# A decoder layer on one core: attention rounds rebuilt on head-centred values, with the decays computed a round earlier

## The reference

```
x1 = norm(x + out_proj(norm(scan(x))))        # selective scan, 16 states a channel
x2 = norm(x1 + attention(x1, ctx))            # 4 heads of 32, causal within a sequence of 64
out = norm(x2 + experts(x2))                  # 8 experts, the best 2 of them per token
```

```
log_D = cs[s] - cs[t] + ig[t]   (t <= s, else -inf),   D = exp(log_D - rowmax)
C     = (q @ k.T / sqrt(32)) * D
h     = (C / max(|sum_t C|, exp(-rowmax))) @ v
h     = (h - mean(h)) * rsqrt(var(h) + 1e-5) * outnorm
```

## Time and profile before

| | us |
|---|---|
| median of 3 runs | 712.76 |
| the three runs | 712.76, 706.27, 712.81 |
| the profiled execution | 705.29 |
| its span | 703.7 |
| PE, DVE, ACT, POOL busy | 539.9, 436.6, 319.9, 359.9 |
| mean granted TensorE clock | 0.869 |

### The profile page before, as it was taken

How to read it: one execution, slowest core, us unless ns; L and a number is a source line. 1 busy time by engine, 2 the same in 40 slices (tenths; PEclk the granted TensorE clock), 3 DMA queues, 4 the chain that set the end, 5 groups by cost and what they waited for, 6 DMA issues and landing times.

```text
span 703.7 us, 10811 instructions
## 1 busy us (share of the span) xinstructions
PE 539.9 (77%) x3387; PEld 381.7 (54%) x3387; DVE 436.6 (62%) x912; ACT 319.9 (45%) x700; POOL 359.9 (51%) x293
## 2 busy tenths in 40 slices
PE   3689999899889797686463879797876689899800
PEld 0234435445344456575353768676665568899800
DVE  1599999999999861676748366656451612212155
ACT  2475575866757444122133345454532423333327
POOL 1497978988779651215516163535352533322341
PEclk9999999999999996555565799998998989999955
DMA  4324435355354513733441735461615247789594
GB/s 148 150 99 148 176 122 189 123 170 177 116 190 146 183 50 67 133 67 62 88 113 36 184 133 157 140 234 37 220 52 187 80 151 244 244 276 287 199 240 122
DMA packets 83320, 104.52 MB, mean 149 GB/s; under 512 B 40784, under 2 KB 64592, under 8 KB 83136
## 3 DMA queue, kind: packets, MB, share of 16 engines
q1 hardware_dynamic: 74576, 90.99, 42.4%
q0 software_dynamic: 4320, 8.92, 3.7%
q10 hardware_dynamic: 4368, 3.93, 2.0%
HBM read 91.48 MB, written 12.34 MB: 148 GB/s over the span
## 4 chain that ended last, share of the span: by engine, by line
issue 27%; PE 20%; DVE 16%; POOL 13%; DMA 10%; SPq 3%; ACT 2%; another core or an unknown queue 1%; ACTq 0%; POOLq 0%; DVEq 0%
POOL hc L634 7%; PE pB L1054 6%; DVE h L1489 6%; DMA wslot<-in_expert_w 5%; PE pq L1067 4%; PE py L809 3%; DVE u L1480 3%; POOL y_dram L737 2%; POOL xg_dram L728 2%; ACT x_all L1439 1%; PE pC L988 1%; DMA y_dram<-dx,xin 1%; POOL dx L621 1%; DMA x_all<-y_dram 1%; PE pq L862 1%
## 5 line engine op out<-in xcount | busy, mean ns | idle before, releaser
L634 POOL TENSOR_TENSOR hc<-h,Crep 128x1024 f32<-128x1024 f32 x64 | 149.5, 2355 | 20.8 <-DVE h L1489 19.8
L737 POOL DMA_INDIRECT y_dram<-dx,xin x71 | 68.7, 968 | 153.4 <-ACT dx L1361 144.3
L1054 PE MATMUL pB<-Crep,wslot 128*128 128x256 f32 (+1 forms) x556 | 118.2, 358 | 21.9 <-DMA wslot<-in_expert_w 10.5
L809 PE MATMUL py<-hc,ident 128*128 128x512 f32 x256 | 121.1, 600 | 6.2 <-POOL hc L634 6.2
L1054 PEld LDWEIGHTS pB<-Crep,wslot 128*128 128x128 f32 x556 | 90.6, 204 | 38.6 <-DMA wslot<-in_expert_w 13.1
L1480 DVE TENSOR_TENSOR u<-dx,pC 128x1024 f32<-128x1024 f32 x64 | 77.1, 1205 | 11.7 <-PE pC L798 11.6
L1784 DVE TENSOR_TENSOR Crep<-u,pB 128x512 f32<-128x512 f32 x35 | 24.1, 687 | 85.3 <-PE pB L1054 48.0
L809 PEld LDWEIGHTS py<-hc,ident 128*128 128x128 f32 x256 | 47.3, 191 | 52.4 <-issue 38.8
L1489 DVE TENSOR_TENSOR_SCAN h<-pB,u 128x1024 f32<-128x1024 f32 x32 | 73.1, 2284 | 0.8 <-ACT pB L1187 0.6
L1489 DVE TENSOR_TENSOR_SCAN h<-pa,u 128x1024 f32<-128x1024 f32 x32 | 73.1, 2283 | 0.0
L1784 DVE TENSOR_TENSOR u<-u,pB 128x512 f32<-128x512 f32 x36 | 24.8, 688 | 77.8 <-PE pB L1054 47.1
(11 more groups left out here) (224 smaller groups left out, 950.8 us busy)
## 6 DMA issues: line engine op xcount, KB each, us to landing
wslot<-in_expert_w SPq DMA_DIRECT2D x46, 768.0 KB
Crep<-c_dram SPq DMA_DIRECT2D x64, 512.0 KB, 3.7
h<-m_dram SPq DMA_DIRECT2D x16, 256.0 KB
xin<-xg_dram SPq DMA_DIRECT2D x25, 130.0 KB
cT_st<-in_ctx_T SPq DMA_DIRECT2D x8, 256.0 KB, 4.0
dx<-in_ctx_T SPq DMA_DIRECT2D x8, 256.0 KB, 4.9
delta<-in_ctx_tok SPq DMA_DIRECT2D x32, 64.0 KB
hc<-y_dram SPq DMA_DIRECT2D x8, 256.0 KB, 8.4
```

The lines of the kernel that those rows point to most:

```text
L634: nc.gpsimd.tensor_tensor(hc[:, K % 4], h[:, K % 3], Crep[:, K % 4].rearrange("p a t -> p (a t)"), ALU.mult).then_inc(hc_done, 1)
L737: nc.gpsimd.indirect_dma_start(out=y2_dram, out_offset=bass.IndirectOffsetOnAxis(ap=xin[:, i % NX, a, D:D + 1].bitcast(i32), axis=0), in_= ...
L809: last = nc.tensor.matmul(py[:], ident[:], hc[:, K % 4, i * CH:(i + 1) * CH], start=False, stop=(K % STEPS == STEPS - 1 and i == 1))
L1054: last = nc.tensor.matmul(bank[:, o * a * P:(o + 1) * a * P], wslot[:, i % NW, stage * F + f * P:stage * F + (f + 1) * P], xgT[i % 2][:, 0 ...
```

## The change

- **Centred values.** The mean of a head is taken out of the values before they are weighted. PE multiplies ctx by a constant centring matrix (`hcenter`, `head_values`), ACT copies the result into `V1` (`copy_values`). The direct loads of the values (`load_v`, four DMAs a chunk) are gone. Since the weighted values are centred already, `normalize` needs no mean: it multiplies by `outnorm` straight from PSUM, ACT squares from PSUM (`square_heads`), and the two row factors are put together in small operations.
- **x2 on ACT.** The last step of `normalize` (four 128x128 operations on DVE, L1645) becomes one small DVE operation (`nma`) and four activations on ACT (`normal_x2`).
- **Decays one round ahead.** `weight_decay(c + 2)` stands at the end of round c on ACT, after `z2_scale` and `normal_x2`. Before, `weight_decay(c + 1)` stood in its first half. For chunks 0 to 4 the gate is added inside the exponential, as a bias: 16 activations of 64 columns in place of one of 1024 and of the DVE addition. For chunks 5 to 7 DVE still adds.
- **First chunk in the last scan chunk.** Chunk 0's buffers move into the expert weights' space (`flatw`). Its ctx and maxima are loaded during the last scan chunk, its mask is made by POOL between the last two `weigh_state`, and its scores and weighted values stand earlier on PE.
- **Weights at the front.** `weights` stands directly behind the first parts of `normalize` on DVE, and the scores and weighted values come sooner on PE. Logits and ranks move from a bank of `pC` into `pa`, and no longer wait for `normalize` to have read `pC`.

```diff
+            def load_m(c):
+                sp.wait_ge(m_stored, 16 * (1 if c < GATED[0][1] else 2))
+                if c == 1:
+                    sp.wait_ge(hc_done, STEPS * NCH)
+                elif c:
+                    sp.wait_ge(causal_done, c)
...
+                    if c + 1 == NCH and k == 1:
+                        load_heads(0)
+                    if c + 1 == NCH and k == 6:
+                        store_m(0)
+                    if c + 1 == NCH and k == 7:
+                        load_m(0)
...
             for c in range(NCH):
                 for k in range(STEPS):
                     weigh_state(STEPS * c + k)
+                    if c + 1 == NCH and k == 6:
+                        start_mask(0)
...
+            def head_values(c):
+                pe.wait_ge(heads_loaded, 16 * (c + 1))
...
+                for b in range(TB):
+                    last = nc.tensor.matmul(pC[:, 0, b * P:(b + 1) * P], cTc[late(c)][:, b * P:(b + 1) * P], hcenter[:],
+                                            start=True, stop=True)
...
             def turn_x2(c):
                 pe.wait_ge(x2_done, c + 1)
                 if c:
-                    pe.wait_ge(x2T_copied, c)
+                    pe.wait_ge(ranks_read, c)
...
             def logits(c):
...
-                pe.wait_ge(hv_done, min(c + 2, NCH))
...
             def weight_decay(c):
-                act.wait_ge(log_decay_done, c + 1)
-                if c:
+                act.wait_ge(causal_done, c + 1)
+                act.wait_ge(g_made, 1 if c < GATED[0][1] else 2)
...
-                nc.scalar.activation(Dm, lmask, ACT.Exp).then_inc(D_done, 1)
+                if c >= ADDED:
+                    act.wait_ge(gates_added, c - ADDED + 1)
+                    nc.scalar.activation(Dm[1], lmask[1], ACT.Exp).then_inc(D_done, 1)
+                    return
+                for m in range(TB * H):
+                    last = nc.scalar.activation(Dm[late(c)][:, m * S:(m + 1) * S], lmask[late(c)][:, m * S:(m + 1) * S], ACT.Exp,
+                                                bias=g_sb[:, c * TB * H + m:c * TB * H + m + 1])
...
+            def normal_x2(c):
+                act.wait_ge(x2_shift_done, c + 1)
+                act.wait_ge(z2_rstd_done, c + 1)
+                for b in range(TB):
+                    last = nc.scalar.activation(x2_rows(c)[:, b], z2[:, b], ACT.Identity, scale=rstd[:, b:b + 1],
+                                                bias=nma[:, b:b + 1])
...
                 if mid:
                     z2_scale(c)
+                    normal_x2(c)
+                if c + 2 < NCH:
+                    weight_decay(c + 2)
                 expert_units(second[2:])
...
-                mid(0)
+                mid(0, 1, 2)
                 if front:
-                    add_gates(c + 1)
-                mid(1, 2, 3, 4)
+                    weights(c + 1, 0)
+                rt(0)
+                mid(3, 4)
                 expert_units(first[0:1])
-                mid(5, 6)
+                mid(5, 6, 7)
...
-                mid(8)
+                mid(8, 9)
                 rt(7)
-                if front:
-                    weights(c + 1, 1)
+                mid(10)
+                if ADDED <= c + 2 < NCH:
+                    add_gates(c + 2)
                 expert_units(second[0:1])
                 rt(8)
-                mid(9)
+                mid(11)
                 rt(9)
-                mid(10)
+                mid(12)
                 expert_units(second[1:2])
```

More of the change, by code:

```diff
@@ L1643, in normalize @@
                     dve.wait_ge(z2_rstd_done, c + 1)
-                    for b in range(TB):
-                        last = nc.vector.tensor_scalar(x2_rows(c)[:, b], z2[:, b], mv[:, b, 0:1], rstd[:, b:b + 1],
-                                                       ALU.subtract, ALU.mult)
-                    last.then_inc(x2_done, 1)
+                    nc.vector.scalar_tensor_tensor(nma[:], mv[:, :, 0], -1.0, rstd[:], ALU.mult, ALU.mult).then_inc(x2_shift_done, 1)
             done = [0]
```

303 lines of the change are left out of this document (164 added, 139 removed).

## The result

The change makes the kernel slower. Its four executions took 722.44, 721.61, 723.75 and 725.0 us, median **723.1**, against 711.56 for the kernel before beside them. The ratio is 1.0229, with a 95% interval of 1.0176 to 1.0283. Forecast were 713 and a range of 699 to 723.

The account below looks back on a forecast made before the run. Bound by a loop over several engines from round 3, and mostly DVE in rounds 0 to 2. Entry -3.0, rounds 1 and 2 0, round 3 -0.6, rounds 4 to 7 +7.2: 709.3 + 3.6 = 713 us, range 699 to 723.

Parts of the forecast that it names:

- Entry: Up to round 1's x2T copy: earlier mask and weighting of chunk 0, less added work; -3.0 us, bounds -8 and +2.
- Rounds 1 and 2: From round 1's x2T copy to round 2's idx: DVE's savings offset by ACT's sixteen exponentials; 0, bounds -7 and +5.
- Round 3: `share` comes earlier and none of ACT's new work lies ahead of idx; -0.6 us, bounds -1.1 and 0.
- Rounds 4 to 7: Second halves: x2 and exponential on ACT between units 1 and 2; 2.3 us each in 4 and 5, 1.3 in 6 and 7.
- The first halves: Later `turn_x2` and DVE's wait in `weights(c+1, 1)` hidden by POOL's sends; 0, or 1 to 2 us a round uncovered.
- Covered by the POOL sends: First halves: the added waits cost 0 because POOL is issuing indirect DMAs; without that, 1 to 2 us a round.
- the sentence on that wait: First halves: `weights(c+1, 1)` waits on DVE for the fourth head's scores, with `route` and products of units 2 and 3 behind.
- The clock rival: Second halves, rounds 5 to 7: PE waits longer for weights and falls to the lower clock; 7.5 us, 720.5, chance 0.17.
- 503.09: Time in round 7 when weights land for PE in the profile before; PE ran at full 2.4 GHz after a 2.07 wait.
- DVE's relief pays: Rival: early rounds follow DVE's shorter work, 3.5 us each in rounds 1 and 2, exponentials hidden; 701, chance 0.28.
- What would show it: The prediction's list of trace signs for and against it, such as idx of round 2 at 335 to 341.
- The first unit of rounds 5 to 7 at 3.8: Sign against the forecast: eight matmuls of the unit at 3.8 us, where 1.99 was seen after a 2.07 wait.

Follow-up runs that it names:

- scores_spread: Changed kernel with the next chunk's head scores and weights spread over the first half as before the change; 712.6 us, ratio 1.0101 to the kernel before.
- changed_again: The changed kernel itself, unedited, run once more beside the edits; 717.4 us, ratio 1.0193 to the kernel before.
- before_again: The kernel before the change, unedited, run again for a second trace; 706.5 us.
- x2_decay_spread: Changed kernel with x2's last step on DVE, the decay exponential at the round's end, scores and weights spread as before; 703.3 us, ratio 0.9984.
- x2_on_vector: Changed kernel with x2's last step back on DVE instead of four ACT activations; 708.7 us, ratio 1.007 to the kernel before.
- fill_second: Changed kernel with 8 unread matmuls in the second half, behind the fourth unit's first product; 720.9 us, ratio 1.0204 to the kernel before.

## Why the prediction was wrong, by its steps

- **Entry, -3.0.** Right: -4.3, inside its bounds. The x1T copy came at 284.56 (forecast 287.4). From it to the x2T copy took 16.6 (15.0). These are two misses that partly cancel, so that the total fits this well is luck.
- **Rounds 1 and 2, 0.** Too low by 2.4, and inside the bounds. The loop from copy to copy took 19.6 where the sum gave 18.6. The exponentials were right; what the sum lacked is DVE's wait for the fourth head's scores, 2.95 in round 1 at 309.20, in rounds that have no sends to cover it. `scores_spread`, where it waits 0.52 and x2 stays on ACT, shortens that loop to 17.4. From the second copy to idx took 17.5, where the sum gave 15.6, with a stall of 3.18 on PE in it. In `changed_again`, without the stall, it took 16.4.
- **Round 3, -0.6.** +0.3, no matter.
- **Rounds 4 to 7, +7.2.** This step failed. The direct part was right: round 4 came out at +1.9, and in round 5 of `changed_again` the silu of unit 2 follows ACT's copy behind unit 1 by 6.53 (439.69 to 446.22), before by 4.56 (436.86 to 441.42), so 2.0 later where 2.3 was forecast. Its error was to end the sum at idx. The two pieces open a wait of 2.34 on PE (0.36 before), PE comes into the next round at half clock, and that is paid again in the first half, through the scatter between the sends. Undoing both gave 10.0 us, x2 alone about 8.7 (the difference of two ratios, 0.0123 of 704.5).
- **The first halves, 0.** This failed too. "Covered by the POOL sends" counted the length of the cover and not what PE does under it. In the kernel before, scores and weighted values stood behind the fourth unit, in the gap where PE waits for weights (428.74 to 430.42 in round 5, and then 1.99). The change moved them forward. The gap opened to 2.66 in the same round of `changed_again`, and the unit took 3.54. Moving them back alone gave 6.5 us, though the product then still took 3.78 in rounds 5 and 6: there PE waits for the rows instead, 2.67 and 2.43. In the first trace the stall of 5.16 came on top, through DVE's order, as the sentence on that wait had feared.
- **The clock rival, 0.17 and 720.5.** This is what happened, with its place (rounds 5 to 7) and almost its price; the result is 2.6 above it, and in `changed_again`, without the stall, rounds 5 to 7 lost 13.2 against `before_again`, where it gave 4.9 and 7.5. Its reason was only half right. It let PE idle longer because the first half gets shorter. That is so in round 7 (the rows are waited for 4.33, before 0.86) and in `x2_decay_spread` and its repeat (3.4 to 5.8). In rounds 5 and 6 PE reached the end of its first half no sooner: in `changed_again` its fourth unit starts 17.0 after idx in round 5, before 16.9. There the gaps came from ACT's work and from the moved scores. I set 503.09 against the rule of the Trainium skill, "TensorE: Matmul & The Clock Gate", section "What's actually happening" (the lower clock is the default, and activity releases it). One product at full clock behind a wait of 2.07 was too little against it: the rule decided, by the granted clocks of 0.80 to 0.84 here and of 1.00 where the gap was filled.
- **DVE's relief pays (0.28).** Wrong for the change as it stands: DVE's busy time in round 1 fell by 5.3 and the round did not follow. The 12.4 and 9.1 us that `x2_decay_spread` and its repeat gain up to round 4 show that the early rounds could follow, once x2 is off ACT and the scores are spread.
- **What would show it.** Of its signs, idx of round 2 (338.2), no gap on ACT and the sixteen exponentials came as forecast. "The first unit of rounds 5 to 7 at 3.8" was the sign against it, and came in rounds 6 and 7 (3.63 and 3.78). In round 5 the trace merges twelve matmuls, 3.88 long, where twelve at full clock take 3.00.

**Not settled.** How the 16.9 of rounds 5 to 7 divide between clock, ACT and stall is known only roughly. Without stalls these rounds took 121.6 against 108.4 in the second trace of the kernel before. Removing ACT's pieces, filling the gaps and spreading the scores overlap, so their gains do not add up. Nor does the length of a wait tell which clock follows: in rounds 5 and 6 of `x2_on_vector` the second half's first product took 1.99 behind waits of 2.42 and 1.99, in round 7 of the first trace 3.78 behind 1.58. The stalls depend on the group: one chip had them in the third and not in the fifth. What causes them was not found.

## What to carry to other kernels

Work that another engine adds inside a chain can cost more than its own length when it leaves TensorE idle: price the next unit at both clocks, and look at which matmuls used to fill that gap before moving them. A gap that has to stay, because a transfer is behind it, can be filled with unread matmuls, but how far they reach matters. Here it paid where they stood ahead of both the rows and the weights and ended within 2 us of each; ending 1.8 to 4.1 us ahead of the rows with none ahead of the weights gave nothing, and overrunning the weights by 2 us took the gain back. Trace the changed kernel more than once before building on one wait.

## What the runs showed of the hardware

- Signals of PE can arrive late while POOL issues indirect DMAs: 1.6 to 10 us, in two of six groups of runs (that of before and after, and the third), and for DVE and ACT at the same moment (418.66 and 418.71). The kernel before has them at the same six places in both. The longest were in a kernel with added matmuls, but partly ahead of the first of these. That it is PE's signal that is late is argued from who waited, not shown.
- Half clock costs more than the slow matmuls. In round 5 of `changed_again` the first product took 1.7 longer (3.62 for 1.89), and the scatter between the sends passed it on: with that product at 1.89, in `fill_second`, the second half began 2.1 sooner after idx.
- Some 160 matmul records of work that nobody reads (36 in 4.18 us) made the kernel about 8 us faster, by ratios of two groups.
